# An attention and expert kernel: the last pair's calls spread over slots 0 to 12, ten record loads given to GpSimd, addresses and Gelu's table set ahead

## What is computed

```
x = x + xattn(layernorm(x), ctx)          # scores scaled by (|q| + |k|)^2, softmax, Wo
logits = layernorm(x) @ Wr                # 8 experts, best two, softmax over the two
h = gelu(x @ W1[e] + b1[e]);  y = h @ W2[e] + b2[e]
x = x + sum over the two experts of share * y
```

## Time and profile before

| what | us |
|---|---|
| median of 3 runs (lowest, highest) | 968.32 (965.58, 971.52) |
| the execution profiled | 970.74 |
| its span, first to last instruction | 968.9 |
| busy in the span: PE, DVE, ACT, POOL | 898.1, 697.2, 634.5, 415.5 |

### The profile page before, as it was taken

The page is one execution under the profiler, slowest core; times in us unless marked ns, Lnnn a source line. Parts: engine busy times, 40 slices in busy tenths (PEclk is TensorE's granted clock), DMA queues, the critical chain, the costliest instruction groups (busy, mean ns, idle before and its releaser), DMA issues.

```text
span 968.9 us, 30634 instructions
## 1 busy us (share of the span) xinstructions
PE 898.1 (93%) x10701; PEld 789.8 (82%) x10701; DVE 697.2 (72%) x1833; ACT 634.5 (65%) x1236; POOL 415.5 (43%) x540
## 2 busy tenths in 40 slices
PE   3999999998999999989899699899999999999994
PEld 2788887787877877878777589799999999999993
DVE  7677888777987887779768577766666666666662
ACT  3688887787877877878857356455555455554551
POOL 6344456538546565385253532623222232222322
PEclk9799999999999999999979799999999999999998
DMA  5222122314132333253044773443333233332222
GB/s 150 70 72 89 41 83 80 112 41 128 57 99 76 126 123 103 92 171 111 20 139 134 275 273 52 85 93 52 51 52 51 47 52 52 52 51 48 46 30 22
DMA packets 61892, 84.82 MB, mean 88 GB/s; under 512 B 9872, under 2 KB 55312, under 8 KB 59568
## 3 DMA queue, kind: packets, MB, share of 16 engines
q1 hardware_dynamic: 47504, 64.26, 21.0%
q0 software_dynamic: 13296, 18.00, 11.1%
q10 hardware_dynamic: 944, 0.60, 0.2%
HBM read 49.86 MB, written 31.92 MB: 84 GB/s over the span
## 4 chain that ended last, share of the span: by engine, by line
PE 74%; issue 7%; DVE 6%; ACT 6%; POOL 3%; another core or an unknown queue 1%; DMA 1%; DVEq 0%; POOLq 0%; ACTq 0%
PE s_ps L711 10%; PE u_ps L711 10%; PE pv_ps L729 9%; PE gen L729 9%; PE gen L502 5%; PE gen L495 5%; PE s_ps L485 5%; PE u_ps L473 3%; PE pv_ps L519 2%; PE gen L544 2%; ACT pt L827 2%; PE gen L415 2%; PE gen L680 2%; PE gen L418 2%; PE gen L422 1%
## 5 line engine op out<-in xcount | busy, mean ns | idle before, releaser
L1567 POOL DMA_INDIRECT out<-yw,rb x71 | 110.3, 1553 | 269.4 <-DVE yw L1392 253.4
L928 ACT ACTIVATE h<-s_ps,b1t,inv 128x128 f32<-128x128 f32 x288 | 107.8, 457 | 89.6 <-PE s_ps L711 79.3
L928 ACT ACTIVATE h<-u_ps,b1t,inv 128x128 f32<-128x128 f32 x280 | 104.7, 459 | 87.4 <-PE u_ps L711 86.4
L1375 DVE TENSOR_SCALAR hs<-h,hsc 128x512 f16<-128x512 f32 x142 | 69.7, 491 | 120.4 <-ACT h L928 102.0
L827 ACT ACTIVATE pt<-gen,escale 128x512 f32<-128x512 f32 x128 | 86.8, 686 | 50.4 <-PE gen L502 34.5
L1377 DVE SCALAR_TENSOR_TENSOR hs<-h,hsc,hs 128x512 f16<-128x512 f32 x142 | 106.7, 751 | 5.1
L711 PE MATMUL s_ps<-xt,w1s 128*128 128x128 f16 x1728 | 104.8, 220 | 2.2 <-issue 2.2
L1517 POOL DMA_INDIRECT xrec<-rec,idx x64 | 77.8, 1215 | 60.9 <-DVE idx L1229 44.7
L711 PE MATMUL u_ps<-xt,w1s 128*128 128x128 f16 x1680 | 102.5, 220 | 0.9 <-issue 0.9
L711 PEld LDWEIGHTS s_ps<-xt,w1s 128*128 x1728 | 99.8, 99 | 2.8 <-issue 2.3
L729 PE MATMUL pv_ps<-w2s_sb,hs 128*128 x864 | 100.5, 272 | 0.5 <-issue 0.5
(11 more groups left out here) (251 smaller groups left out, 1741.8 us busy)
## 6 DMA issues: line engine op xcount, KB each, us to landing
wl<-L_ffn_W SPq DMA_DIRECT2D x16, 1024.0 KB
rb<-xrec SPq DMA_DIRECT2D x71, 132.5 KB
w2s<-wst SPq DMA_DIRECT2D x8, 1024.0 KB
w2s_sb<-w2s SPq DMA_DIRECT2D x8, 1024.0 KB, 20.4
xin<-x SPq DMA_DIRECT2D x32, 128.0 KB, 3.5
cin<-ctx SPq DMA_DIRECT2D x32, 128.0 KB, 2.1
xres<-x SPq DMA_DIRECT2D x32, 128.0 KB
out<-x SPq DMA_DIRECT2D x30, 128.0 KB, 2.0
```

Of the source, the lines that this page charges most:

```text
L928: ins = act.activation(h32[n % HBANKS][:, m % HB, :], hbank[n % HBANKS][:, o:o + SLOT], ACT.Gelu, scale=inv1[:, bass.ds(ex, 1)].bitcast(F3 ...
L1567: pool.indirect_dma_start(out[:, :], bass.IndirectOffsetOnAxis(ap=rb[j][:, D + NE:D + NE + 1], axis=0), yw[s % 2][:, :], None, compute_op= ...
```

## The change

Everything is in the second stage and where the stages meet.
- SP: `b2s` is loaded first; ten records instead of nine are loaded; `store_w2` of the last matrix comes after the first two matrices are back, five matrices are fetched before it and three after it; the loads of slots 10 to 19 are taken out.
- POOL: `add(s)` for s from 1 to 10 loads the records of slot s + 9 after its wait for `add(s - 1)` and before its own DMA. The last pair's scatters stand behind adds 9 to 12 instead of 5 to 8.
- PE: slot 0 is transposed before the last pair's `project_out`; the addresses of slots 0 to 2 are set ahead; the last pair's calls are spread to slots 0 to 7. From slot 60 on a first product is made one slot ahead of its second product instead of two.
- ACT: an activation of one column with Gelu's function stands right behind the first stage. The first Gelu waits for `inv1` alone. The last pair's calls stand behind gelu(1), gelu(2), gelu(5) and gelu(7).
- DVE: the first two copies come before `residual` and the scales; `weight_low(15)` moves into slot 0; `residual(1)` to slot 1, `choose`, `counts`, `shares`, `positions`, `last_tables` to slots 5, 6, 8, 9, 10.

```diff
 sync
+            for b in range(2):
+                sp.wait_ge(*at(f"v{b}", NP))
+            sp.dma_start(b2s[:, :, :], b2.partition_broadcast(P)).then_inc(sig("ldb2"), 16)
             sp.wait_ge(*at("soon", 1))
             sp.wait_ge(*dma("scat", 4 * (SOON_PAIR + 1)))
-            for s in range(U - 1):
+            for s in range(U):
                 load_records(s)
-            store_w2(NP - 1)
             sp.wait_ge(*at("pv3", NP))
-            for e in range(NE - 1):
+            for e in range(W2_SOON):
                 load_w2(e)
...
             for e in range(NE):
+                if e == 2:
+                    store_w2(NP - 1)
+                if e == W2_SOON:
+                    sp.wait_ge(*dma("stw", NE))
+                    for late in range(W2_SOON, NE):
+                        load_w2(late)
                 sp.wait_ge(*dma(f"ldw2_{e}", 1))
                 sp.sem_inc(sig("w2_ready"), 1)
-            for s in range(U - 1, SOON):
-                load_records(s)
 tensor
-            def first_product(s, ex):
+            def first_product(s, ex, ahead=()):
...
+                        for address in itertools.islice(ahead, 2 * DC):
+                            pe.to_reg(address)
...
+            experts = [expert_of(pe, 0)]
+            for address in first_addresses(experts[0]):
+                pe.to_reg(address)
+            turn_records(0)
             project_out(0, NP - 1)
+            experts.append(expert_of(pe, 1))
+            turn_records(1)
+            first_product(0, experts[0], first_addresses(experts[1]))
             heads_back(1, NP - 1)
-            for s in range(3):
-                turn_records(s)
-            experts = [expert_of(pe, s) for s in range(3)]
-            first_product(0, experts[0])
+            turn_records(2)
+            experts.append(expert_of(pe, 2))
+            first_product(1, experts[1], first_addresses(experts[2]))
             turn_on(1, NP - 1)
-            first_product(1, experts[1])
-            project_out(1, NP - 1)
-            turn_y(0, NP - 1)
             for s in range(NSLOT):
                 if s + 3 < NSLOT:
                     turn_records(s + 3)
-                if s + 2 < NSLOT:
-                    first_product(s + 2, experts[2])
+                if s + 2 < SHORT:
+                    first_product(s + 2, experts[2], second_addresses(experts[0]) if s == 0 else ())
+                elif SHORT - 2 < s < NSLOT - 1:
+                    first_product(s + 1, experts[1], second_addresses(experts[0]))
                 if s == 0:
+                    project_out(1, NP - 1)
+                if s == 1:
+                    turn_y(0, NP - 1)
+                if s == 2:
                     logits(0, NP - 1)
+                if s == 3:
                     turn_y(1, NP - 1)
-                if s == 1:
+                if s == 4:
                     logits(1, NP - 1)
-                if s == 4:
+                if s == 7:
                     ranks(NP - 1)
 scalar
+            act.activation(gelu_one[:, :], mhalf[:, :], ACT.Gelu)
...
-                    act.wait_ge(*at("scales", 1))
+                    act.wait_ge(*at("inv1", 1))
...
-                if s == 0:
+                if s == 1:
                     o_turned(1, NP - 1)
-                if s == 1:
+                if s == 2:
                     store_x1(0, NP - 1)
                     record_high(0, NP - 1)
-                if s == 2:
+                if s == 5:
+                    store_x1(1, NP - 1)
                     record_high(1, NP - 1)
-                    store_x1(1, NP - 1)
-                if s == 5:
+                if s == 7:
                     route_exp(NP - 1)
 vector
-                if 0 <= it - 1 < NP:
+                if 0 <= it - 1 < NP - 1:
                     weight_low(it - 1)
...
+            take_records(0)
+            dve.tensor_scalar(inv1[:, :], k1[:, :], 25.0, float(ONE), ALU.subtract, ALU.mult).then_inc(sig("inv1"), 1)
+            take_records(1)
+            hidden_scales()
+            experts = [expert_of(dve, s) for s in range(2)]
             residual(0, NP - 1)
-            heads_back(1, NP - 1)
-            take_records(0)
-            take_records(1)
-            experts = [expert_of(dve, s) for s in range(2)]
             split_hidden(0, experts[0])
             take_records(2)
-            residual(1, NP - 1)
+            heads_back(1, NP - 1)
             split_hidden(1, experts[1])
             for s in range(NSLOT):
...
+                if s + 2 < SHORT:
                     split_hidden(s + 2, experts[2])
+                elif SHORT - 2 < s < NSLOT - 1:
+                    split_hidden(s + 1, experts[1])
+                if s == 0:
+                    weight_low(NP - 1)
+                if s == 1:
+                    residual(1, NP - 1)
+                if s == 2:
+                    logits(0, NP - 1)
+                if s == 4:
                     logits(1, NP - 1)
                 weigh(s, experts[0])
...
-                if s == 1:
+                if s == 5:
                     choose(NP - 1)
-                if s == 2:
+                if s == 6:
                     counts(NP - 1)
-                if s == 5:
+                if s == 8:
                     shares(NP - 1)
-                if s == 6:
+                if s == 9:
                     positions(NP - 1)
-                if s == 7:
+                if s == 10:
                     last_tables()
 gpsimd
+            def load_records(s):
+                j = s % U
+                if s >= U + 5:
+                    pool.wait_ge(*dma(f"ldsoon{s % 5}", 1))
+                row = pool.value_load(slot_row[0:1, s:s + 1], min_val=0, max_val=NE * REGION)
+                pool.dma_start(rb[j][:, :], xrec_d[bass.ds(row, SLOT), :]).then_inc(sig(f"ldsoon{s % 5}"), 16)
...
                 if s:
                     pool.wait_ge(*dma(f"add{(s - 1) % U}", (s - 1) // U + 1))
+                    if s - 1 + U < SOON:
+                        load_records(s - 1 + U)
...
-                if 5 <= s < 9:
+                if 9 <= s < 13:
                     for i in range(2):
-                        scatter(s - 5, i, NP - 1)
+                        scatter(s - 9, i, NP - 1)
 constants
+    W2_SOON = 5
+    SHORT = 60
```

More of the change, by code:

```diff
@@ L144, in build @@
     cnt_i = alloc(ctx, "cnt_i", [P, NE], I32)
+    gelu_one = alloc(ctx, "gelu_one", [P, 1], F32)
     s_ps = bank("s_ps", [P, 2, 512], F32)
@@ L673, in turn_records @@
                 g = xt_bank[:, 0:2 * DC * SLOT // 2].bitcast(F16)
-                pe.wait_ge(*dma(f"ldrec{s % U}", s // U + 1))
+                if U <= s < SOON:
+                    pe.wait_ge(*dma(f"ldsoon{s % 5}", 1 if s < U + 5 else 2))
+                else:
+                    pe.wait_ge(*dma(f"ldrec{s % U}", s // U if s >= SOON else 1))
                 if s:
@@ L758, in tensor_program @@
                     experts.append(expert_of(pe, s + 3))
-                later = second_addresses(experts[1]) if s + 1 < NSLOT else ()
-                second_product(s, experts[0], itertools.chain(later, first_addresses(experts[3]) if s + 3 < NSLOT else ()))
+                if s + 3 < SHORT:
+                    ahead = itertools.chain(second_addresses(experts[1]), first_addresses(experts[3]))
+                elif s + 3 == SHORT:
+                    ahead = second_addresses(experts[1])
+                elif s + 2 < NSLOT:
+                    ahead = first_addresses(experts[2])
+                else:
+                    ahead = ()
+                second_product(s, experts[0], ahead)
                 experts.pop(0)
@@ L1335, in vector_program @@
                     logits(1, it - 1)
-            exponent(b1ss[:, :], kb[:, :])
-            step(dve.tensor_scalar(mk[:, :], k1[:, :], 4.0, None, ALU.add))
-            step(dve.tensor_tensor(mk[:, :], mk[:, :], kb[:, :], ALU.max))
-            step(dve.tensor_scalar(mk[:, :], mk[:, :], 1.0, None, ALU.add))
-            step(dve.tensor_scalar(hsc[:, :], mk[:, :], -float(ONE), 268.0 * ONE, ALU.mult, ALU.add))
-            step(dve.tensor_scalar(inv1[:, :], k1[:, :], 25.0, float(ONE), ALU.subtract, ALU.mult))
-            step(dve.tensor_tensor(inv2[:, :], mk[:, :], k2[:, :], ALU.add))
-            dve.tensor_scalar(inv2[:, :], inv2[:, :], 155.0, float(ONE), ALU.subtract, ALU.mult).then_inc(sig("scales"), 1)
-            dve.wait_ge(*at("scales", 1))
             def last_tables():
@@ L1393, in weigh, with hidden_scales @@
                                   None, ALU.mult).then_inc(sig("yw"), 1)
+            def hidden_scales():
+                exponent(b1ss[:, :], kb[:, :])
+                step(dve.tensor_scalar(mk[:, :], k1[:, :], 4.0, None, ALU.add))
+                step(dve.tensor_tensor(mk[:, :], mk[:, :], kb[:, :], ALU.max))
+                step(dve.tensor_scalar(mk[:, :], mk[:, :], 1.0, None, ALU.add))
+                step(dve.tensor_scalar(hsc[:, :], mk[:, :], -float(ONE), 268.0 * ONE, ALU.mult, ALU.add))
```

(25 more changed lines are left out.)

6 lines of the change are left out of this document (removed).

## The result

The changed kernel takes 987.18 us (median of 4 runs, 986.01 to 987.92); the kernel before, beside it, 967.91 us (median of 4, 965.58 to 971.52). The ratio is 1.0195, with a 95% interval of 1.0161 to 1.0228: slower by about 19 us, where 978.8 was forecast and 988 was the upper end. The profiled execution took 986.85 us, its span 985.2 us (970.7 and 968.9 before).

The account below looks back on a forecast made before the run. PE sets the pace at 5.52 us a slot, except where the stages meet, the first dozen slots and the tail. Slot 8's 12.8 us loss less the tail's 2.3 gives +10.5 on 968.3: 978.8 us, range 966 to 988.

Parts of the forecast that it names:

- The start: Where the stages meet: slot 0's copy follows its transposition at once; first second product ends at 556.4, 12.2 us ahead.
- only as a rival: At the start: addresses cost 2.1 us and the clock falls too, 3 us more, 982 us; no chance of its own.
- First new wait: Iteration 1: second_product(1) waits for a chain behind first_product(3); PE 5.4 us idle, plus 1.5 us lost to clock.
- Second: Iteration 4: slot 7's transposition waits because add(0) stands behind record_low(1), record_high(1) and gelu(5); PE 6.1 us idle.
- add(0) isn't held: Rival at iteration 4: POOL has the last record's high half in time, so no second wait; 967.7 us, chance 0.10.
- POOL's chain: add(1) to add(10): a load of 1.7 us plus an add's 4.5 us give a period of 6.2 us, above 5.52.
- Dear loads: Rival on GpSimd: from 3.5 us per load the period is 8 us; 984 to 992 us, chance 0.10.
- Third: Iteration 7: 3.2 us idle for slot 9's copy, then 5.8 us at ranks behind choose, two table loads, gelu(8) and counts.
- 981.7 us: Time if, by the skill page, draining at table switches made the third wait 2.8 us longer.
- Sum at slot 8: PE's second product of slot 8 ends at 626.5 instead of 613.7, 12.8 us behind.
- Behind that: Stage of the last tables: its 5.3 us loss was left unchanged, between none and 8.
- The tail: Last slots: second_product(69) ends 2.6 us ahead of the last, PE's end to last add becomes 4.05 us; 2.3 us gained.

Follow-up runs that it names:

- w2_wait: all_sp, with SP's second to fifth loads of W2 behind the copy of slot 3; 953.22 us, ratio 0.9974.
- on_first: all_sp with DVE's start reordered: heads_back(1) and slot 2's copy ahead of slot 0's split and residual(0); 951.45 us, ratio 0.9962.
- bank_free: on_apart with DVE's residual(0) ahead of the split of slot 0 instead of behind it; 942.98 us, ratio 0.9840 to the kernel before.
- res_early: Changed kernel, but DVE does residual(1) in iteration 0 and ACT record_high(0) behind gelu(3) instead of gelu(2); 980.13 us, ratio 1.0133.
- low_late: Changed kernel, but GpSimd does the last record's low half behind add(4), not ahead of add(0); 977.69 us, ratio 1.0100.
- exp_late: Changed kernel, but ACT does route_exp behind gelu(9) instead of gelu(7); 986.70 us, ratio 1.0194.
- on_apart: on_first with PE's ranks in iteration 8 for 7 and DVE's last_tables in iteration 12 for 10; 946.08 us, ratio 0.9890.
- tail_only: Kernel before with, from slot 60, first products one slot ahead and addresses worked out in the first product; 953.27 us, ratio 0.9971.
- scat_late: tail_only with the last pair's scatters in iterations 9 to 12 for 5 to 8; ratio 0.9977.
- sp_loads: Changed kernel with only the loads of slots 10 to 19 moved back from GpSimd to SP; 970.61 us, ratio 1.0138.
- all_sp: Changed kernel with the moves of low_late, exp_late and res_early, and the loads of slots 10 to 19 back on SP; 955.03 us, ratio 0.9987.

## Why the prediction was right, and where it was short

The forecast was a slower kernel with its losses at named places, and that is what came: 987.2 us lies in the range, 8 us above the forecast. One of its own signs of being wrong came true: the first second product was to end near 556 and not after 560, and it ended at 560.9. So the start was mistaken. The four waits behind it came where they were named, and the wait at the two table loads stands between them, not before them.

- *The start.* Right in kind, a third too good: second_product(0) ends at 560.9, not 556.4 (568.6 before), so 7.7 us ahead instead of 12.2. Slot 0's turn (540.4 for 540.3) and the first product at full clock (2.84 us) were right; the 32 addresses took about 0.8 us for 0.5. The step that failed is "`turn_on` then waits for DVE ... which is 549.4". The wait ended at 552.5, 3.57 us for 1.5. (The terms given there add up to 548.7, not 549.4; summed rightly, the start would have been forecast 0.7 us still further off.) I had let DVE's split begin with Gelu's end, which came at 546.42, as forecast. It began 2.4 us later, at 548.83: DVE had 1.51 us without work, in which it reads two experts' numbers, two steps of 0.65 to 0.70 us on 8 columns, and residual(0) with its statistics ahead of it. w2_wait excludes the four later W2 transfers, and on_first with bank_free shows the order to be the cause: with `heads_back` and the residual ahead of the split the wait is 0.51 us. Behind the wait first_product(2) ran for the most part at half clock, 4.47 us for 2.84; the prediction had named this only as a rival.
- *First new wait.* 6.02 us for 5.4, and 1.7 us of clock for 1.5; the chain was as described, and res_early took it away by breaking it at ACT and DVE.
- *Second.* 5.20 us for 6.1, add(0) behind gelu(5) as said. The rival "add(0) isn't held" falls by low_late: it was held, at a price of 9 us.
- *POOL's chain.* A period of 6.2 us was forecast, and it is 6.0 to 6.5. A load costs 6.1 - 4.5 = 1.6 us (1.7 taken). "Dear loads" falls as a price, yet the chain counts: 5.5 us in the changed kernel, 6.7 us with the other waits gone. The Trainium skill, page "DMA: Bandwidth & Descriptors", section "SWDGE vs HWDGE vs iDMA", advises plain transfers from SP or ACT; the two pairs of runs agree with it here, by these 5.5 and 6.7 us.
- *Third.* 3.05 us for slot 9's copy at the transposition of slot 10, for 3.2, and 4.85 + 0.67 at `ranks` for 5.8. Right in size. That the table for Exp stands in the chain was wrong: it was loaded at 603.63 while ACT waited (below). A gap of 0.52 us ahead of Gelu's table, which the sum lacked, made up part of these 1.28 us, so that this size came out so near is in part luck. (The 981.7 us beside the tables' price are 978.8 + 2.8 = 981.6.) And exp_late shows a limit of the argument: taking this wait away gains nothing while the stage of the tables takes it back.
- *Sum at slot 8.* 17.8 us behind for 12.8: 4.5 of the 5 are the start's.
- *Behind that.* "I leave it" was nearly right: from slot 8 to PE's end 1.2 us less were lost. With the loads gone from GpSimd the wait at the tables was still 2.87 us, and on_apart shows that it comes from DVE's crowded iterations and not from its load.
- *The tail.* 2.7 us for 2.3, and 2.8 by itself in tail_only.
- *Left out.* GpSimd's DRAIN, 2.5 us longer. By the two profiled executions the sum was 5.6 us short (986.85 - 970.74 = 16.1 for 10.5). The other 2.8 of the 8.4 us come from the step to the median: the profiled execution of before lay above its median, that of after 0.3 us below it.

## What to carry to other kernels

Moving work behind a critical step pays only as far as each engine's queue behind the new place is followed to the next buffer: here 6.50 us of PE's waiting went and five other waits came, the dearest by a 0.64 us instruction at the head of GpSimd's queue. When a wait stays after its named releaser has been made early, read the name again: in on_first it had changed from `on` to the residual, that is from data to a bank. And a wait that hides another pays nothing alone, so such edits are judged together (exp_late alone: 0).

## What the runs showed of the hardware that was not expected

- *The table is loaded ahead of the wait.* ACT's load of Exp's table starts at 603.63, the activation it belongs to waits 7.64 us for `rd` and starts at 612.56. So only Gelu's table, 1.28 us, lay in the chain. Gelu starts 1.30 us after that load's start (613.28 and 614.58), as in the earlier trace rows.
- *GpSimd's last DRAIN depends on what its queue did long before.* 3.05 us before and in tail_only; 4.81 us when the scatters stand in iterations 9 to 12 (scat_late, and all kernels with the loads on SP); 5.59 us when ten plain loads are issued there too. The move of the scatters is shown by scat_late as a cause. That the loads make the other 0.78 us is shown by sp_loads against the changed kernel. Why a DRAIN at the end should feel either is open.
- *The clock.* Of the changed kernel's five waits of 3 us or more four end inside a stretch at a granted 0.50, the 1.2 GHz level, or just ahead of one (552.51, 570.20, 591.57, 620.93); behind the one of 3.05 us the first product took 2.84 us. The wait of 1.81 us at `ranks` was followed by such a stretch in all_sp and not in on_first. bank_free, whose longest wait there is 1.30 us, shows 1.00 throughout the windows above. Of its gain of 15.3 us on the kernel before, 9.2 are idle time (gaps of over 0.35 us: 2.77 us for 11.97), and 2.8 the last add's distance to PE's end (3.50 for 6.35), less 1.8 for the DRAIN. That leaves 5.1 us. Some 2 of them are the addresses: the second and third first product of before took 3.94 and 3.84 us at a granted 1.00, and in bank_free they take 2.84 and 2.85. For the other 3 us the 10.2 + 3.4 us that before had at half clock between 540 and 625 are the likeliest cause; that wasn't measured apart.
- *Short DVE steps.* The same step on 8 columns takes 0.17 us in one place and 0.65 to 0.70 in another (543.59 and 544.32 above); in on_apart it is another step of the same chain that takes 0.62. Beside the two steps in the changed kernel GpSimd was at work, and each ended 0.03 to 0.04 us behind GpSimd's instruction:

```profile
543.27 0.98 POOL L1551 DMA_INDIRECT xrec<-rec,idx  x1 [0.17 <-POOL rec L1527]
544.28 0.65 POOL L1527 TENSOR_TENSOR rec<-xn,rec 128x256 f16<-128x256 f32 x1
```

  In all_sp, on_first, on_apart and bank_free too every such step that is stretched beside a low half ends 0.04 us behind it, but most steps beside a scatter take 0.17 us. So GpSimd's work is the likeliest cause; no run took it away.
